# The product with v, four heads at a time or eight heads at a time

## The reference

```python
q, k, v = heads(xm @ Wqkv)                       # 16 heads of 16 columns
scores = einsum('bhqd,bhkd->bhqk', q, k) * scale
attn = softmax(where(mask, scores, -inf), axis=-1)
out = einsum('bhqk,bhkd->bhqd', attn, v)         # the product with v
x = x + gate * (out.reshape(b, t, c) @ Wproj + bproj)
x = x + gate2 * (gelu(norm(x) @ W1 + b1) @ W2 + b2)
```

## Time and profile before

| | |
|---|---|
| median of 3 runs | 1178.01 us (1175.23 to 1180.79) |
| the profiled execution's own time | 1178.39 us |
| its span (first to last instruction) | 1176.2 us |
| PE busy | 1091.0 us, 93% |
| DVE busy | 752.3 us, 64% |
| ACT busy | 622.6 us, 53% |
| POOL busy | 252.9 us, 22% |
| granted TensorE clock, mean | 0.971 |

### The profile page before, as it was taken

One profiled execution on the slowest core, in us unless ns is written; L12 is line 12 of the kernel. 1 busy time (PEld: TensorE's weight loads), 2 busy tenths in 40 slices (PEclk: granted clock), 3 DMA queues, 4 the chain that ended last, 5 costly groups with the idle time before them and its releaser, 6 DMA issues.

```text
span 1176.2 us, 24117 instructions
## 1 busy us (share of the span) xinstructions
PE 1091.0 (93%) x9228; PEld 958.2 (81%) x9228; DVE 752.3 (64%) x1627; ACT 622.6 (53%) x1255; POOL 252.9 (22%) x252
## 2 busy tenths in 40 slices
PE   3989999999999788999985899999999987999998
PEld 3778989998987577899874788888888766988997
DVE  5456666666665457765645687878787646566653
ACT  1146666666665643443331677777777666334431
POOL 5101221211211244223321112121212013121111
PEclk9789999999999999999987899999999999999999
DMA  7547767567561010000057473746456400000001
GB/s 214 114 70 118 129 114 119 97 110 124 135 101 23 7 55 10 13 10 11 14 85 159 72 96 64 97 65 96 70 91 77 58 2 1 19 33 22 19 19 36
DMA packets 50826, 81.49 MB, mean 69 GB/s; under 512 B 8916, under 2 KB 23476, under 8 KB 49620
## 3 DMA queue, kind: packets, MB, share of 16 engines
q1 hardware_dynamic: 49752, 78.37, 37.5%
q10 hardware_dynamic: 960, 1.57, 1.2%
HBM read 22.64 MB, written 8.44 MB: 26 GB/s over the span
## 4 chain that ended last, share of the span: by engine, by line
PE 83%; DVE 4%; DMA 4%; SPq 3%; ACT 2%; issue 2%; POOL 2%; ACTq 1%; POOLq 0%; DVEq 0%
PE g_bank L541 14%; PE st_bank L541 13%; PE o_bank L629 9%; PE o_bank L541 8%; PE s_bank L541 7%; PE s_bank L596 6%; PE st_bank L615 5%; PE s_bank L590 3%; PE st_bank L609 3%; PE st_bank L611 3%; PE s_bank L592 2%; PE g_bank L687 2%; SPq L406 2%; DMA k_stack<-qk_split 2%; DMA q_stack<-negmaxT 1%
## 5 line engine op out<-in xcount | busy, mean ns | idle before, releaser
L807 ACT ACTIVATE probs<-st_bank 128x384 f32<-128x384 f32 (+1 forms) x512 | 273.6, 548 | 156.5 <-PE st_bank L611 89.9
L910 ACT ACTIVATE probs<-st_bank,cols 128x512 f32<-128x512 f32 x128 | 88.0, 689 | 217.6 <-PE st_bank L541 191.1
L541 PE MATMUL st_bank<-qk_split,q_stack 128*128 128x512 f32 x768 | 187.3, 402 | 15.4 <-ACT probs L910 10.8
L1099 DVE TENSOR_REDUCE maxima<-s_bank 128x2 f32<-128x512 f32 x256 | 168.9, 685 | 42.5 <-PE s_bank L596 41.6
L541 PEld LDWEIGHTS st_bank<-qk_split,q_stack 128*128 128x128 f32 x768 | 144.8, 191 | 53.0 <-ACT probs L910 13.8
L1095 DVE TENSOR_REDUCE maxima<-s_bank 128x3 f32<-128x384 f32 x256 | 138.7, 554 | 60.1 <-PE s_bank L592 56.9
L596 PE MATMUL s_bank<-k_stack,q_stack 97*128 97x256 f32 x512 | 115.9, 309 | 17.8 <-DMA k_stack<-mask_dram 10.6
L541 PE MATMUL g_bank<-xmT,wa 128*128 128x256 f32 x768 | 122.7, 299 | 4.8 <-POOL xmT L1271 4.8
L629 PE MATMUL o_bank<-probs,v_sb 128*32 128x256 f32 (+1 forms) x2048 | 124.7, 361 | 1.6 <-ACT probs L807 1.6
L596 PEld LDWEIGHTS s_bank<-k_stack,q_stack 97*128 97x128 f32 x512 | 80.1, 195 | 44.4 <-issue 28.0
L1271 POOL TENSOR_TENSOR xmT<-xm_full,xmT 128x512 fp32r<-128x512 f32 x32 | 42.3, 1322 | 331.8 <-ACT xmT L873 331.8
(11 more groups left out here) (114 smaller groups left out, 2104.7 us busy)
## 6 DMA issues: line engine op xcount, KB each, us to landing
q_stack<-qk_split SPq DMA_DIRECT2D x192, 128.0 KB, 4.5
k_stack<-qk_split SPq DMA_DIRECT2D x180, 128.0 KB, 6.0
gate_rows<-gate_dram SPq DMA_DIRECT2D x32, 128.0 KB, 3.4
w_dram<-w_in SPq DMA_DIRECT2D x8, 512.0 KB, 7.2
wm_f32r<-w_dram SPq DMA_DIRECT2D x4, 1024.0 KB, 7.9
out<-x_sb SPq DMA_DIRECT2D x8, 512.0 KB, 2.9
x_sb<-x_in SPq DMA_DIRECT2D x4, 512.0 KB, 7.8
k_stack<-qk_split ACTq DMA_DIRECT2D x12, 128.0 KB, 8.7
```

The lines of the kernel that those rows point to most:

```text
L541: last = mm(dst, weights[i], rows[j], start=(f == 0 and n == 0), stop=(f == tiles - 1 and n == len(TERMS) - 1))
L807: activation(probs[:, h % 8, 0:n], st_bank[h % 2][:, 0:n], ACT.Exp, scale=SCALE)\
L910: activation(h_full[:, m % 2], st_bank[m % 2][:, :], ACT.Gelu, bias=cols[:, cb + m:cb + m + 1])\
L1099: v.reduce_max(maxima[:, gb.mod(2), 0:2, slot], bank[:].rearrange("p (i n) -> p i n", n=T), AX.X).then_inc(max_done, 1)
```

## The change

`GROUP` becomes 8: `attend` is issued twice a batch, for eight heads, four into the left half of `o_bank` and four into the right. The slots are 12 and 4 in place of 9, 13, 1 and 5. ACT copies the whole bank once for eight heads. The ring of probabilities grows from 8 to 12 heads. The scratch for the descriptors of DMAs that POOL issues goes from 4096 to 1024 bytes; POOL issues none in this kernel.

```diff
-GROUP = 4
+GROUP = 8
 NG = H // GROUP
+QUAD = 4
+NQ = H // QUAD
+RING = 12
-PV_SLOT = [(LAG + 5 + GROUP * i) % H for i in range(NG)]
+PV_SLOT = [(LAG + GROUP * (i + 1)) % H for i in range(NG)]
...
-        probs = sb("probs", [P, 8, 512])
+        probs = sb("probs", [P, RING, 512])
...
+        def ring(g, h):
+
+            return (g.const * H + h) % RING
...
                 wait(pe, o_copied, g.count(NG, r))
                 first = P if layer == 0 else 0
-                for kt in range(NT):
-                    for j in range(GROUP):
-                        h = GROUP * r + j
-                        lo = first if kt else 0
-                        last = mm(o_bank[32 * j:32 * j + 32, lo:T], v_sb[:, g.mod(VBUFS), kt, h, :],
-                                  probs[:, h % 8, kt * T:kt * T + T - lo], start=(kt == 0), stop=(kt == NT - 1),
-                                  tile_position=(0, 32 * j), skip_group_check=True)
+                for u in range(GROUP // QUAD):
+                    for kt in range(NT):
+                        for j in range(QUAD):
+                            h = GROUP * r + QUAD * u + j
+                            lo = first if kt else 0
+                            last = mm(o_bank[32 * j:32 * j + 32, u * T + lo:(u + 1) * T],
+                                      v_sb[:, g.mod(VBUFS), kt, h, :],
+                                      probs[:, ring(g, h), kt * T:kt * T + T - lo], start=(kt == 0),
+                                      stop=(kt == NT - 1), tile_position=(0, 32 * j), skip_group_check=True)
                 last.then_inc(pv_done, 1)
...
-                    wait(act, pv_done, g.count(NG, h // GROUP - 1))
+                    wait(act, pv_done, g.count(NG, (h - RING) // GROUP + 1))
...
-                    activation(o_sb[:, g.mod(2), r, :], o_bank[:, 0:T], ACT.Copy).then_inc(o_copied, 1)
+                    activation(o_sb[:, g.mod(2), 2 * r:2 * r + 2],
+                               o_bank[:].rearrange("p (u n) -> p u n", u=GROUP // QUAD), ACT.Copy).then_inc(o_copied, 1)
...
-    nc = bacc.Bacc("TRN2", target_bir_lowering=False, num_devices=1, dynamic_dma_scratch_size=4096)
+    nc = bacc.Bacc("TRN2", target_bir_lowering=False, num_devices=1, dynamic_dma_scratch_size=1024)
```

More of the change, by code:

```diff
@@ L154, in build @@
         negmaxT = sb("negmaxT", [32, T], f32r)
-        o_sb = sb("o_sb", [P, 2, NG, T])
+        o_sb = sb("o_sb", [P, 2, NQ, T])
         rsum = sb("rsum", [P, 2, H])
@@ L685, in step @@
                         bank = take(layer, t, f"oT{i}")
-                        for r in range(NG):
+                        for r in range(NQ):
                             last = transpose(bank[:, r * P:(r + 1) * P], o_sb[:, gd.mod(2), r, i * P:(i + 1) * P],
@@ L711, in step @@
                         r = PV_SLOT.index(s)
-                        g, on = (gc, c) if LAG + 5 + GROUP * r < H else (gd, d)
+                        g, on = (gc, c) if LAG + GROUP * (r + 1) < H else (gd, d)
                         if on.within(B):
@@ L804, in exponentials @@
                     act.wait_ge(st_ready, g.count(H, h + 1))
-                    wait(act, pv_done, g.count(NG, h // GROUP - 1))
+                    wait(act, pv_done, g.count(NG, (h - RING) // GROUP + 1))
                     n = 3 * P if layer == 0 else 4 * P
-                    activation(probs[:, h % 8, 0:n], st_bank[h % 2][:, 0:n], ACT.Exp, scale=SCALE)\
+                    activation(probs[:, ring(g, h), 0:n], st_bank[h % 2][:, 0:n], ACT.Exp, scale=SCALE)\
                         .then_inc(exp_done, 1)
```

## The result

The changed kernel takes 1213.95 us (median of 4 runs, 1207.82 to 1214.51) against 1177.32 us before on the same terms: ratio 1.0299, 95% interval 1.0263 to 1.0335. It is 3.0% slower. The forecast was 1203 us, in a range from 1187 to 1216; the result lies in that range, but above the 1195 to 1210 that the forecast case had given for itself.

A forecast was written before the change was run, and what follows sets the result against it. PE, busy throughout full steps, was taken as the bound; 1178.4 - 22.4 saved at the ends + 11.4 + 16.5 + 15.0 + 3.3 of waits = 1202.2, plus 1 for starts and drains: 1203 us, range 1187 to 1216.

The forecast's parts named there:

- the forecast case: Switch savings outweighed by three waits: 1203 us, own range 1195 to 1210, chance 0.64.
- The ends: PE pays 0.35 us at a product group's two ends; eights save 0.70 us a step, -11.2 us in each layer.
- The maxima's way: Slot 1, PE waits for negmaxT DMAs once the group leaves: 0.7 and 1.07 us a step, +11.4 and +16.5 us.
- The attention output: Slot 11, L695 waits for DVE's output halves: 1.15 us a step in layer 1, +15.0 us; layer 0 none.
- The modulation behind the copy: Slot 12, ACT's copy delays the modulation, q projection waits 0.25 us a step in layer 1: +3.3 us; layer 0 none.
- The sum: Whole kernel: savings and waits give 1202.2 us, with starts and drains 1203 us, 2% slower.
- the starts and drains: Short steps at each layer's start and drain wait for whatever is late: put at +1 us.
- That eight cost twice four: Rival: nothing is saved at the product groups' ends, 1225 us, chance 0.04.
- That only the maxima are late: Rival: only the maxima's way is late, DVE finds room by reducing ahead, 1187 us, chance 0.14.
- the rival in which the waits push one another: Rival: waits add another 1 us in each full step of layer 1, 1216 us, chance 0.10.

The follow-up runs named there:

- without maxima: Changed kernel with the maxima unused (scoresT reads 97 rows, head 0 does not wait for the DMAs; another softmax): 1175.49 us, ratio 0.9973 to before.
- hybrid: Kernel before, regrouped as one group of eight heads in slot 13 and two of four in slots 1 and 5: 1176.83 us, ratio 0.9999.
- slot 10 run: Changed kernel with DVE's normalisation of the next batch in slot 10 in place of slot 7: 1210.36 us, ratio 1.0262 to before.
- slot 5: Changed kernel with its second group of eight in slot 5 in place of slot 4 (slots 12 and 5): 1203.24 us, ratio 1.0217 to before.
- pair of runs without it: Changed kernel and kernel before, each without the use of the maxima (another softmax): 1175.49 us and 1172.12 us.
- slot 13: Changed kernel with its groups of eight in slots 13 and 5 in place of 12 and 4: 1198.16 us, ratio 1.0181 to before.
- the ring alone: Kernel before with only the ring of 12 heads and the smaller scratch, groups and slots as before: 1175.46 us, ratio 0.9985.
- all in eights, three moves: Changed kernel, eights in slots 13 and 5, normalisation in slot 6, output before head 9's reduction, maxima transposed in slot 0: 1182.24 us, ratio 1.0035 to before.

## Why the prediction was right

- *The ends.* Forecast 0.70 us a step. Layer 0 gives 0.64 (20.74 without maxima) and 0.33 for one pair (hybrid). In layer 1, what is left of the changed step without its waits, 22.19 - 1.08 - 1.10 - 0.36, is 19.65: 0.5 saved, less than the 0.70. A group of eight lasts 1.93 us as forecast; by starts it adds 0.20 us ahead of it in slot 4, where the wait stands right before (0.09 with the maxima unused), and 0.10 behind.
- *The maxima's way.* Forecast 0.7 and 1.07 us a step; measured 0.75 and 1.08 to 1.16. Right in place, price and cause, by the pair of runs without it.
- *The attention output.* Forecast 1.15 in layer 1 and 0 in layer 0; measured 1.10, and none in layer 0's full steps. The slot 10 run took its 0.65 us off. What the forecast did not see is the shorter chain behind it, which kept slot 5 from being a full cure.
- *The modulation behind the copy.* Forecast 0.25 (the terms as they stand, 5.63 against 5.43, give 0.20); measured 0.30 by starts, 0.36 by the step that slot 13 shortened. The Trainium skill's rule on breaking up instructions ("Perfetto Trace Analysis", section "Optimizing Scalar/DVE Operations") was not tried by itself: no run here splits the copy, and the wait went with the group's move to slot 13.
- *The sum.* A full step of layer 0 was forecast at 21.4 (21.49), of layer 1 at 21.9 (22.19). Measured is 36.6 us, forecast 25. The 13 steps of layer 1 account for 13 x 0.27 = 3.5 us of the difference, mostly the ends' saving taken too high, and those of layer 0 for up to 2. The term that was mis-sized is the starts and drains, put at +1 beyond the waits counted there: the drains alone are 5 us longer, and the stretches outside the steps 3 more. In the drains PE waits 2.21, 2.64, 2.16 and 2.68 us for the DMAs of the maxima, 9.7 in all, where it waited 6.5 before; the kernels with slots 12 and 5, 13 and 5, and slot 10 repeat each of the four within 0.01 us. In layer 0's drain PE's busy time grew too, from 57.8 to 60.5 us, at a mean clock of 0.90 in place of 0.97. That drains get longer is the change's: the two together take 135.4 and 133.9 us in the profiles of before and of the ring alone, and 140.6 to 145.4 in those of the changed kernel and its three relatives. Why the clock falls there more, and the 3 us elsewhere (1.8 ahead of the first transposition of the maxima, where the ring alone has 2.0 with the same work on PE, and 1.5 in the last MLP), stay open.
- *The rivals.* That eight cost twice four is refuted by layer 0. That only the maxima are late is refuted by the slot 5 run. The time, 1213.95, lies next to the 1216 of the rival in which the waits push one another, but that rival wanted a further 1 us in each full step of layer 1, and the step is 0.27 over the forecast. The verdict is right by its mechanism; that the time fell within the range owes something to the upper bound that this rival had set, since the excess over 1203 came from elsewhere: the starts and drains, and the ends' smaller saving.

## What to carry to other kernels

On an engine that is busy all the time, a block's place in the list is worth as much as its length: look for what the others do while it runs, and how long that takes from its first start to its last end, before taking it away. Such a way (here 4 us through ACT, SP and two DMAs) shows no wait in a full step's profile as long as it is covered; with only some 0.15 us of slack here, nearly all of the 1.22 us of work taken out of it came back as a wait. When a merge saves a little per step, merge the blocks that cover nothing and leave those that do, and start the long ways earlier first.

## What the runs showed of the hardware

Going from products on the whole array to products on quarters of it and back costs PE 0.33 us for the pair of ends: layer 0's step went from 21.38 to 21.05 with one pair fewer and to 20.74 (maxima unused) and 20.71 (all in eights, three moves) with two. The Trainium skill says that changing the tiling mode drains the engine ("TensorEngine Tiling (Array Packing)", section "Key Properties"); the runs agree with a cost at the ends, and give the price, though none separates the switch itself from what else a group brings. The overhead per matmul that the same page names ("Instruction Overhead") would have given no saving.

The granted clock fell from 2.4 to 1.2 GHz in work that followed some of the waits in the drains: in the changed kernel 0.50 after the wait of 2.64 us (388.30), in the kernel before 0.51 after one of 1.53 us. It did not after one of 2.51 us in the kernel before. So the length of the last wait alone does not tell whether the clock falls. Rows of the changed kernel, then of the one before:

```profile
390.40:396.60 6.20, 6.18 (x33) 5.82 (x30) 1.37 (x4) 3.32 (x7) 0.00 (x0) 0.50 0.00 0
```

```profile
365.19 0.39 PE L609 MATMUL st_bank<-q_stack,k_stack 99*128 99x256 f32 x1 [1.53 <-DMA q_stack<-negmaxT]
402.49 0.66 PE L695 MATMUL g_bank<-ident,attn 128*128 128x128 f32 x4 [2.51 <-DVE attn L1122]
...
402.60:411.00 8.40, 5.44 (x34) 4.64 (x35) 4.92 (x12) 7.82 (x22) 0.75 (x1) 1.00 0.00 1
366.40:369.60 3.20, 3.20 (x26) 2.44 (x27) 0.83 (x2) 1.28 (x3) 0.00 (x0) 0.51 0.00 0
```

The two waits of 1.1 us inside the dense steps of layer 1 left the clock at 1.00 in each of the 12 full steps. Where it fell, the wait cost more than its own length: with the maxima used, layer 0's drain of the changed kernel has 4.7 us more of idle time and 4.6 us more of busy time; in the kernel before (clock 0.97 with and without) it has 4.1 us more of idle time and 0.3 of busy time.
